# Attention on one core: each group of heads takes its second 512 queries before its first 512, and the bias is added to x in four pieces

## The reference

```python
q, k, v = x @ Wq.T + bq, x @ Wk.T + bk, x @ Wv.T + bv     # 16 heads of 8
scores = einsum('bqhd,bkhd->bhqk', q, k) * attn_scale
# a query in a chunk of 64 does not see keys of earlier chunks, nor later places of its own chunk
attn = softmax(where(mask, -inf, scores))
x = layernorm(x + (attn @ v) @ Wo.T + bo)
w = top 6 of 32 experts, out of the best 4 of 8 groups, normed, * 2.5
x = layernorm(x + sum_e w_e * (silu(x @ G_e.T) * (x @ U_e.T)) @ D_e.T + shared(x))
```

## Time and profile before

| what | us |
|---|---|
| median of 3 runs | 442.95 (442.84 to 443.32) |
| the profiled execution | 443.64 |
| its span in the trace | 441.6 |
| PE busy in the span | 408.4 (92%) |
| DVE busy | 343.2 (78%) |
| ACT busy | 227.3 (51%) |
| POOL busy | 134.3 (30%) |

### The profile page before, as it was taken

How to read it: one execution, slowest core, us unless ns; L and a number is a source line. 1 busy time by engine, 2 the same in 40 slices (tenths; PEclk the granted TensorE clock), 3 DMA queues, 4 the chain that set the end, 5 groups by cost and what they waited for, 6 DMA issues and landing times.

```text
span 441.6 us, 8085 instructions
## 1 busy us (share of the span) xinstructions
PE 408.4 (92%) x2864; PEld 213.8 (48%) x2864; DVE 343.2 (78%) x776; ACT 227.3 (51%) x309; POOL 134.3 (30%) x254
## 2 busy tenths in 40 slices
PE   6659999999999999999989979999999999999992
PEld 2324334343333334334334436766776776666660
DVE  4959978898989898989954555976778768778863
ACT  4610077784878696877777775232432253332220
POOL 5000714665465666566554150000000000000000
PEclk9955569999999999999999999999999999999998
DMA  4565024020302112020000015333223332424530
GB/s 121 190 203 161 4 79 135 25 89 6 107 4 82 33 54 60 23 78 6 3 2 4 1 35 115 107 113 98 91 91 106 86 112 95 126 95 126 134 99 24
DMA packets 27391, 34.51 MB, mean 78 GB/s; under 512 B 5912, under 2 KB 16472, under 8 KB 27352
## 3 DMA queue, kind: packets, MB, share of 16 engines
q1 hardware_dynamic: 27016, 33.34, 25.3%
q10 hardware_dynamic: 336, 0.66, 0.6%
HBM read 29.33 MB, written 4.65 MB: 77 GB/s over the span
## 4 chain that ended last, share of the span: by engine, by line
PE 76%; DVE 8%; ACT 4%; SPq 3%; DMA 3%; POOL 2%; issue 2%; ACTq 1%; DVEq 0%; POOLq 0%
PE ps L1231 16%; PE ps L1329 13%; PE ps L1188 10%; PE ps L1300 7%; PE ps L1302 7%; PE ps L1301 7%; PE ps L1212 7%; DVE mx L900 5%; ACT probs L798 3%; PE ps L1192 3%; PE ps L1254 2%; SPq L539 2%; POOL x L738 1%; DVE oT L883 1%; DMA ebias<-in_ebias 1%
## 5 line engine op out<-in xcount | busy, mean ns | idle before, releaser
L900 DVE TENSOR_REDUCE mx<-ps 128x1 f32<-128x512 f32 (+3 forms) x304 | 179.6, 657 | 24.5 <-PE ps L1192 20.3
L798 ACT ACTIVATE probs<-ps 128x1024 f32<-128x1024 f32 (+2 forms) x160 | 143.6, 940 | 52.0 <-PE ps L1212 50.8
L1188 PE MATMUL ps<-rows_k,rows_q 48*128 48x512 bf16 (+3 forms) x384 | 103.2, 362 | 11.7 <-DMA rows_k<-scratch 7.6
L840 ACT ACTIVATE rows_q<-ps 128x512 f32<-128x512 f32 x68 | 40.8, 599 | 94.5 <-PE ps L1302 92.3
L1231 PE MATMUL ps<-probs,Vg 128*32 128x512 f32 (+3 forms) x768 | 82.5, 502 | 0.3 <-POOL probs L702 0.3
L1300 PE MATMUL ps<-x1hi,w_hi 128*128 128x512 f32 x136 | 73.4, 540 | 2.7 <-ACT probs L798 1.6
L1212 PE MATMUL ps<-rows_q,rows_k 51*128 51x512 bf16 (+3 forms) x384 | 71.7, 335 | 2.8 <-ACT probs L798 2.1
L1329 PE MATMUL ps<-rows_q,w_down 128*128 128x512 f32 x136 | 69.5, 593 | 0.8 <-DVE rows_q L1127 0.8
L1122 DVE TENSOR_TENSOR rows_k<-ps,rows_q 128x512 f32<-128x512 f32 x64 | 43.9, 687 | 33.1 <-PE ps L1329 32.6
L1188 PEld LDWEIGHTS ps<-rows_k,rows_q 48*128 48x128 bf16 x384 | 30.1, 96 | 81.2 <-DVE mx L900 65.1
L698 POOL TENSOR_SCALAR_AFFINE_SELECT probs<-probs 64x512 f32<-64x512 f32 x64 | 42.3, 661 | 83.2 <-ACT probs L798 82.4
(11 more groups left out here) (101 smaller groups left out, 328.1 us busy)
## 6 DMA issues: line engine op xcount, KB each, us to landing
comb_rows<-weights SPq DMA_DIRECT2D x128, 128.0 KB, 3.0
scratch<-oT SPq DMA_DIRECT2D x8, 384.0 KB, 3.5
w_raw<-in_unitT SPq DMA_DIRECT2D x17, 128.0 KB, 2.4
rows_q<-scratch SPq DMA_DIRECT2D x16, 96.0 KB
rows_k<-scratch SPq DMA_DIRECT2D x14, 96.0 KB
w_down<-in_unitT SPq DMA_DIRECT2D x1, 1088.0 KB, 6.1
xT<-in_xT SPq DMA_DIRECT2D x4, 256.0 KB, 4.1
rows_q<-scratch SPq DMA_DIRECT2D x16, 64.0 KB
```

The lines of the kernel that those rows point to most:

```text
L798: act.activation(dst, src, ACT.Exp).then_inc(exps_ready, 1)
L900: dve.tensor_reduce(dst, src, AX.X, ALU.max).then_inc(max_read, 1)
L1188: mm = pe.matmul(bank(max_bank(k), m, at), q, rows_k[r0:r0 + ROWS_QK, s, j * T + k0:j * T + k0 + m], start=True, stop=not first, tile_posi ...
```

## The change

The four blocks, 12 maxima units and the top of a group's second 512 queries now come first in all three streams; tile 7's two shared units move with them, so part 1 has 12 units and part 0 has 26. The top comes 5 units into the next part, not 4. The maximum over tile 3's two pieces (the join, L903) is taken after the first unit of the next group. `nth_top` numbers the tops in their new order, so that the semaphore counts fit. In a group, the units of expert weights and the values of the next group are still split or made behind selects of the first 512 queries' blocks, which now stand later in the group. The values of group 1 are made like those of the others, behind a select of group 0. The bias is added to x in four pieces of four tiles, behind the first and third of those selects in group 0 and the second in groups 1 and 2 (`BIAS_BEHIND`).

```diff
--- before.py
+++ after.py
@@ -43,6 +43,13 @@
 PART_KEYS = HG * KT // 2
+PART_ORDER = (1, 0)
+
+
+def nth_top(g, part):
+
+    return 2 * g + PART_ORDER.index(part)
+
 
@@ -57,7 +64,7 @@
                 units += [[(j, qt, k0, m, 0, k0 == P * qt)] for j in range(2)]
-    if part == 0:
+    if part == 1:
         units.append([(j, q, P * last if q == last else P * q + BANK, P, b * 2 * P + j * P, q == last)
@@ -69,14 +76,14 @@
     for g in range(NG):
-        for part in range(2):
+        for part in PART_ORDER:
             units = [("unit", g, part, cells, half_) for cells in max_cells(part) for half_ in range(2)]
...
 
-TOP_AFTER = 4
+TOP_AFTER = 5
 MAX_RING = 3
@@ -92,12 +99,12 @@
     lower = [kt for pair in zip(range(KT - 1, KT // 2 - 1, -1), range(KT // 2 - 1, -1, -1)) for kt in pair]
-    return [(kt, 0) for kt in lower] + [(kt, 1) for kt in range(KT - 1, KT // 2 - 1, -1)]
+    return [(kt, 1) for kt in range(KT - 1, KT // 2 - 1, -1)] + [(kt, 0) for kt in lower]
 
...
 NB = len(BLOCKS)
-LOWER = KT
+LOWER = KT // 2
 QCOLS = [P * (kt + 1) - BANK if h else min(BANK, P * (kt + 1)) for kt, h in BLOCKS]
@@ -142,8 +149,9 @@
 
-POOL_RANK = {"first": 0, "split": 1, "values": 2, "unit": 3, "mask": 4}
-BETWEEN_MASKS = [c for c in range(LOWER) if DIAGONAL[c]][:3]
+BIAS_BEHIND = ((0, 0), (0, 2), (1, 1), (2, 1))
+POOL_RANK = {"first": 0, "split": 1, "values": 2, "bias": 2, "unit": 3, "mask": 4}
+BETWEEN_MASKS = [c for c in range(LOWER, NB) if DIAGONAL[c]][:3]
 
@@ -162,7 +170,7 @@
     act_todo, pe_order, act_order, masks_before = [], [], [], []
-    pool_todo, pool_order, joined = [("first", 0, 0, 0.0, 1500)], [], {}
+    pool_todo, pool_order, joined = [("first", 0, 0, 0.0, 750)], [], {}
     tt = [(0, n) for n in range(len(FIRST_TAIL))]
@@ -201,8 +209,10 @@
                 k = BETWEEN_MASKS.index(n) if n in BETWEEN_MASKS else -1
-                if k == 1 and 1 <= g and g + 1 < NG:
+                if k == 1 and g + 1 < NG:
                     pool_todo.append(("values", g + 1, 0, pool, 750))
+                if (g, k) in BIAS_BEHIND:
+                    pool_todo.append(("bias", g, BIAS_BEHIND.index((g, k)), pool, 1150))
                 if k >= 0 and 3 * (g - 1) + k in range(NU):
@@ -270,9 +280,9 @@
                 m_done[n] = dve
-                if n - 1 == LAST_OF[g, 0]:
+                if n - 1 == LAST_OF.get((g - 1, 0)) or n == LAST_OF[NG - 1, 0]:
                     dve += 150
-                    joined[g] = dve + hop
+                    joined[g if n == LAST_OF[NG - 1, 0] else g - 1] = dve + hop
             else:
@@ -607,11 +617,11 @@
                 s = g % NS
-                sp.wait_ge(max_split, 2 * g + part + 1)
+                sp.wait_ge(max_split, nth_top(g, part) + 1)
                 r0 = g % GPB * STRIP + 2 * part
...
                 sp.dma_start(region.rearrange("h c (q p) -> (c q) h p", p=P), mh[:, part, :, :]).then_inc(max_stored, 16)
-                sp.wait_ge(max_stored, 16 * (2 * g + part + 1))
+                sp.wait_ge(max_stored, 16 * (nth_top(g, part) + 1))
                 for half_ in range(2):
@@ -627,10 +637,10 @@
             for g in range(NG):
-                store_max(g, 0)
+                store_max(g, 1)
                 if g == 0:
                     load_rows(2)
-                store_max(g, 1)
+                store_max(g, 0)
                 if g == 0:
@@ -720,9 +730,9 @@
                 if g >= 1:
-                    pool.wait_ge(max_stored, 16 * (2 * g + part - 1))
-                n, top = 3 * (2 * g + part), mn[:, part, :]
-                pool.wait_ge(tops_copied, 2 * g + part + 1)
+                    pool.wait_ge(max_stored, 16 * (nth_top(g, part) - 1))
+                n, top = 3 * nth_top(g, part), mn[:, part, :]
+                pool.wait_ge(tops_copied, nth_top(g, part) + 1)
                 pool.tensor_copy(mh[:, part, 0, :], top).then_inc(max_split_steps, 1)
@@ -734,11 +744,13 @@
                 values(0)
+
+            def bias(n):
                 pool.wait_ge(tail_consts_loaded, 16 * 5)
-                pool.tensor_tensor(x[:, :, :], x[:, :, :], bob[:, :].unsqueeze(1).to_broadcast([P, NT, C]),
+                quad = x[:, QUAD * n:QUAD * (n + 1), :]
+                pool.tensor_tensor(quad, quad, bob[:, :].unsqueeze(1).to_broadcast([P, QUAD, C]),
                                    ALU.add).then_inc(x_biased, 1)
-                pool.wait_ge(x_biased, 1)
-                values(1)
+                pool.wait_ge(x_biased, n + 1)
 
@@ -748,6 +760,8 @@
                     values(g)
+                elif kind == "bias":
+                    bias(n)
                 elif kind == "unit":
@@ -800,13 +814,14 @@
                 if g >= 1:
-                    act.wait_ge(max_split, 2 * g + part - 1)
-                act.wait_ge(tops_ready, 2 * g + part + 1)
+                    act.wait_ge(max_split, nth_top(g, part) - 1)
+                act.wait_ge(tops_ready, nth_top(g, part) + 1)
                 act.activation(mn[:, part, :], bank(max_bank(k), P)[0:PART_KEYS, :], ACT.Copy,
...
 
-            def copy_output(g, h):
-                act.wait_ge(values_used, NB * g + (NB if h else LOWER))
+            def copy_output(g, second):
+                h = 0 if second else 1
+                act.wait_ge(values_used, NB * g + (NB if second else LOWER))
                 act.copy(oT[:, g, h * BANK:(h + 1) * BANK], bank(VALUES)).then_inc(output_copied[h], 1)
@@ -888,7 +903,7 @@
                 if g >= 1 and k in PART_STARTS:
-                    dve.wait_ge(tops_ready, TOPS_THROUGH[k] if part else 2 * g - 1)
+                    dve.wait_ge(tops_ready, 2 * g - 1 if part else TOPS_THROUGH[k])
                 dve.wait_ge(max_scores, READS_THROUGH[k])
@@ -898,8 +913,8 @@
                 dve.tensor_reduce(dst, src, AX.X, ALU.max).then_inc(max_read, 1)
-                if part == 1 and k == LAST_OF[g, 0] + 1:
-                    dve.wait_ge(max_read, READS_THROUGH[k - 1])
+                if k - 1 == LAST_OF.get((g - 1, 0)) or k == LAST_OF[NG - 1, 0]:
+                    dve.wait_ge(max_read, READS_THROUGH[k if k == LAST_OF[NG - 1, 0] else k - 1])
                     dve.tensor_tensor(maxima_of(0)[0], maxima_of(0)[0], maxima_of(2)[0],
@@ -911,7 +926,7 @@
             dve.tensor_tensor(gate_lo[:, :], gate_w[:, :], gate_hi[:, :], ALU.subtract).then_inc(gate_split, 1)
-            dve.wait_ge(x_biased, 1)
+            dve.wait_ge(x_biased, NC)
 
@@ -1221,9 +1236,9 @@
                     if g >= 1:
-                        pe.wait_ge(output_copied[1], g)
+                        pe.wait_ge(output_copied[0], g)
                 elif c == LOWER:
-                    pe.wait_ge(output_copied[0], g + 1)
+                    pe.wait_ge(output_copied[1], g + 1)
                 pe.wait_ge(exps_ready, NE * g + EXPS_UP_TO[c])
@@ -1244,7 +1259,7 @@
                 else:
-                    pe.wait_ge(output_copied[1], NG)
+                    pe.wait_ge(output_copied[0], NG)
                 if kind == "out":
```

## The result

The changed kernel takes 454.61 us (median of 4 runs, 449.33 to 457.98) against 443.13 us: 1.0146 times the time before, 95% interval 1.0091 to 1.0200. The forecast was 442.5, 439.3 to 446.0.

A forecast was written before the change was run, and what follows sets the result against it. PE at half clock and DVE equally limit the early maxima; PE's order sets the steady part. Start +0.2 and end -0.2 make 0 on profiled 443.64, 0.69 above the median; 442.95 less 0.4 for TOP_AFTER gives 442.5, range 439.3 to 446.0.

The forecast's parts named there:

- The first top and the first exponentials: Start of attention: top transposed at 36.4, split by 38.8, exponentials at 45.7 after PE waits 0.7 us.
- The ledger at the start: PE's work done by 64.3, in microseconds at full clock: 19.5 against 19.7 before, so 0.2 us lost.
- gap with maxima only: Between group 0's two exponential starts, 56.6 to 63.8: PE has only maxima, 12 to 13 units, 7.2 us.
- By the first distance the clock rises at 53.7: Start: PE's clock rises 8.0 us behind the first exponential, as before, leaving 4.0 us of ledger work at half clock.
- the clock falls in the gap: Rival: maxima alone let the clock fall; exponentials restart at half clock for 8 us, costing 4 us: 446.5; chance 0.12.
- The rival of the second top being late: POOL or SP delays group 0's second top; PE waits behind the gap, 2 us, 444.5; chance 0.11.
- The end: End of attention: join +0.3, output copy -0.59, 128 more queries on ACT +0.3 and PE +0.24, hidden selects -0.3.
- Sum about -0.2: Net forecast for the end of attention, from join, output copy, extra queries and hidden selects: about -0.2 us.
- The experts' first matmul: Behind attention: PE's first matmul of the experts forecast at 260.7.
- The bias: Bias pieces and group 1's values on POOL: put at nothing, with 0 to 2 us possible if selects are delayed.
- The steady period: Middle groups: PE's order only shifted, period stays 25.05 us, 0 taken; 0.15 us a group either way is 1 us.
- TOP_AFTER: Top after 5 units takes transposes off the reduction: 0.05 us for each of 16, half PE's, so -0.4 us.

The follow-up runs named there:

- e13: e1 with the combination weights' transpose on PE and copy on ACT moved late, as the new order has them: 448.80 us, 1.0079 of before.
- e8: The kernel before, with POOL starting the whole bias only behind DVE's first join: 444.02 us, 0.9973 of before.
- e15: The changed kernel run again unaltered, on another chip: 451.74 us, 1.0122 of before.
- e2: The changed kernel with ACT taking the first two Silu steps right behind its last exponential: 445.82 us, 1.0022 of before.
- e11: e2 with the top 4 units into the next part, not 5: 447.25 us, 1.0036 of before.
- e7: The changed kernel with the bias whole again, so the order alone is changed: 459.49 us, 1.0322 of before.
- e1: The kernel before with only the bias in four pieces and group 1's values behind a select, old order: 443.64 us, 0.9958 of before.
- e4: The kernel before with 8 filler matmuls in PE's idle stretch near the start: 445.56 us, 0.9999 of before.
- e5: e1 with 8 f32 fillers in PE's idle stretch and one behind each maxima unit until the first exponential: 452.18 us, 1.0151 of before.
- e3: The changed kernel with 8 filler matmuls in PE's idle stretch near the start: 450.87 us, 1.0106 of before.
- e10: e2 with 8 f32 fillers in PE's idle stretch, then light bf16 ones up to the first exponential and in the gap: 446.78 us, 1.0035 of before.
- e12: e1 with the top 5 units into the next part, not 4: 445.80 us, 1.0021 of before.
- e14: e12 with the first two Silu steps right behind ACT's last exponential: 441.68 us, 0.9911 of before.
- e6: e2 with the f32 fillers of e5 before the first exponential and also in the gap: 454.50 us, 1.0185 of before.

## Why the prediction was wrong

**The first top and the first exponentials**: right. Top at 35.95 (36.4 forecast), split from 36.77 to 38.39 (38.8), first exponentials on PE at 45.80 (45.7), having waited 0.39 us for the rows (0.7).

**The ledger at the start**: its layout was right (gap with maxima only, second start at 66.3, forecast 63.8), its clock wrong. "By the first distance the clock rises at 53.7" took a time from the earlier trace rows as if the clock counted time since the first exponential. The runs show no fixed distance: in the old order the clock rose from 4.6 us (e13) to 11.0 us (e8) behind ACT's first exponential. Of the five profiles of the new order with no filler, it did not rise before the gap in two, both of the changed kernel (up at 73.1, and at 73.4 in e15). In the other three it rose 7.9 to 8.9 us behind the first exponential and fell again in the gap (e2: 55.3 and 62.1; e11: 54.6 and 61.4; e7: 63.7 and 70.5). So the rival "the clock falls in the gap", with 0.12, was the true mechanism in three of five, and the changed kernel's own profiles are worse than it. Its price of 4 us for 8 us at half clock was twice too high: a microsecond at half clock behind the first exponential was worth about 0.25 us in e1, e4, e5 and e8. But e15 has 18.7 us more of them than e1, an estimated 4 to 5 us from these numbers, more than the 2.7 by which it is late at the last exponential. Together with e3 and e10 this points to the clock, and not to the order, as what makes the start and middle late; it rests on one profile of each run. The rival of the second top being late did not come true: the split was done at 58.3, and PE did not wait at 66.34.

**The end**: this step failed most. "Sum about -0.2" counted an output copy, 128 queries and a join, and never asked where the planner would put the steps of the tail (the work behind attention) among the last blocks. In the new order the router's weights came behind PE's last exponential scores and not ahead of them (262.93 in e15, 257.17 before); the planner placed their transpose behind two values blocks and two experts' groups, and ACT, which takes the Silu steps only with the last output copy, waited. Measured by itself in the old order (e13): +5.2 us in place of -0.2. Taking it out of the new order (e2) gives back 4.4 by ratios. That is more than half of the loss of 5 to 8 us by which e15 stands above before and e1. The experts' first matmul, forecast at 260.7, came at 264.1 (e15: 263.5).

**The extra falls of the clock** were in no term of the sum. One lies in the end's wait (274.5 to 288.2). Two others came at 192.6 and 264.3, where PE had been busy for 3.83 and 2.26 of the 4 us before. The one at 192.6 cost 1.6 us: from one top to the next, 190.57 to 208.90, it was 18.33 us, against 16.77 in e15 (191.50 to 208.27), which has no such fall; e2, with one at 191.8, took 18.38. The next top did not make it up. Here half clock cost nearly half of its 3.4 us. The runs with the lower mean clocks are mostly the longer ones (e15: 447.64 us at 0.946, 456.60 at 0.925).

**The bias**: "I put them at nothing" was right as a cost. What it missed is the gain: the whole bias at times blocked the join for 4.4 us in the kernel before. The four runs that before was first given by all lay from 442.84 to 443.82, so the stated result holds none of this, and the later ratios do (e1's 0.9958). In the changed kernel the join still ran 0.23 to 0.68 us in five of its seven later groups and not 0.17 (before: in one of seven, 0.33); what held it there is not shown.

**The steady period** was right: four groups, from the top at 91.30 to that at 191.50, took 25.05 us each in e15, as forecast.

**TOP_AFTER** was given -0.4 for the step from 4 to 5. In the old order e12 was 2.2 us above e1 at the end, though 1.2 us ahead of it at the last exponential; e14, 2.0 us below e1, has the Silu steps moved as well, so what the top's place is worth there is not shown. In the new order 5 was the worse choice: e2 was 4.6 us behind e11 at the last exponential, 1.6 of them by the clock.

## What to carry to other kernels

When several streams are woven by a planner, a change of order moves steps at both ends. Read, for the last ten microseconds, what each engine has next in its written order and on which engine that waits, and tie no step (here two Silu steps) to another that it does not need. A large instruction on GpSimd that reads SBUF can stop a tiny one on VectorE that has two SBUF inputs; a kernel whose runs fall into two groups is worth a profile of the slower group. A piece of work brought forward is worth only what fills the place behind it: here 1280 of 4608 columns, and then the gap.

## What the runs showed of the hardware

Matmuls of 48 rows, with their masks of 64, did not raise the granted clock from 1.2 to 2.4 GHz in 28 us of full PE, and at 2.4 GHz, with PE busy for 2.74 of 4 us, they let it fall (e4: at 30.2). One f32 matmul of 128 x 128 by 128 columns behind each unit held it for the same maxima in e5's profile, but not always: in e6's profile the clock fell at 29.0 with the same fillers, and one of e5's six runs had a mean clock of 0.924. The Trainium skill, page "TensorE: Matmul & The Clock Gate", section "A second HAM failure mode: psum-queue depth-cycling", names short idle times between groups; e4's fall agrees with that, while the 28 us of maxima without a rise had hardly any idle time (27.4 of 28.4 us busy) and are not covered by it. A 128 x 128 by 128 f32 filler cost 0.42 us of PE at full clock. What a microsecond at half clock costs depends on the stretch: nothing with maxima alone (16.91 against 16.92 us for 29 reductions), about 0.25 us behind the first exponential (1.8 us for 7.3), nearly 0.5 in the steady part (1.6 us for 3.4). And a DVE instruction of 0.17 us stood for 4.43 us beside a GpSimd one.
